# Two-layer graph attention kernel on one core: count plans read ahead, the attention fold's weights loaded by head, the second projection's first block in other banks, one eviction a chunk earlier

## The chip, the cores and the metric

The kernel runs on one core of a Trainium2 chip, in one launch. The metric is the device time of an execution in microseconds, lower is better. Three executions of the kernel before took 921.67, 923.18 and 926.49 us.

## The reference

Two graph attention layers over 1250 nodes of 768 values and 20000 edges (plus one self loop a node), a residual and a layer norm:

```
def _gat_layer(x, src, dst, W, a_src, a_dst, bias, concat):
    h = (x @ W).reshape(N, H, C)
    al_s = einsum('nhc,hc->nh', h, a_src);  al_d = einsum('nhc,hc->nh', h, a_dst)
    e = leaky_relu(al_s[src] + al_d[dst], 0.2)
    ex = exp(e - segment_max(e, dst)[dst])
    alpha = ex / (segment_sum(ex, dst)[dst] + 1e-16)
    out = segment_sum(h[src] * alpha[:, :, None], dst)
    ...                                   # heads side by side, or their mean
h   = elu(_gat_layer(x, src, dst, W1, att_src1, att_dst1, b1, concat=True))   # 4 heads of 512
out = _gat_layer(h, src, dst, W2, att_src2, att_dst2, b2, concat=False)       # 1 head of 768
return layernorm(x + out)
```

## The kernel before, in words

There is no gather. The edges are counted into a dense matrix C of 1250 x 1250 (source block x target), and each layer is a dense product: for a source block of 125 nodes and a half of the targets (a *chunk*, 125 x 625) the weights exp(...) x counts are made, split into a high and a low part, and multiplied with the rows of h, each product in three passes (high x high, high x low, low x high). Each engine runs its own list of instructions written out by hand, and semaphores order them; there is no scheduler. The stages in the order of TensorE's list (`block.tensor`):

1. *Fold*: W1 is transposed in 16 steps (`fold_step(i)`, four a head: six transposes, L1791, then two products of the step before with the attention vectors, L1801). ScalarE copies the transposes out (`weights_out`, L1102). Ten steps (`FS`) stand ahead of the counts, the rest between the first count windows. `w1f` holds W1 for this; the sync engine SP issues its loads as 12 DMAs of two heads each. ScalarE makes its share of the one-hots (`slot_ones`, L1062 and L1065) before its first `weights_out`.
2. *Counts*: 30 windows of 41 or 42 targets. VectorE makes one-hots (`one_hots`, L1422, seven a step), TensorE multiplies them (`window`, L1854 to L1863, in a loop whose trip count is data), ScalarE copies the counts out (`strip_out`, L1077) and makes the table for a later window (`shift_table`, L1071). Where a window's slots start and how many steps it takes is computed on VectorE (`plan_row`, semaphore `ranges`) and read into registers of TensorE and of VectorE by `windows_plan`, one read (L567) for four windows (`WQ`). The first `Q0` = 4 reads stand ahead, on TensorE ahead of the first fold step; those for windows 16, 20, 24 and 28 stand in the loop over windows. Between the windows stand transposes of x (L1822), score rows, count transposes (`transpose_counts`, L1872, with ScalarE's `mask_out`, L1085) and, from window 24 on, the split of W1's first head (ScalarE L1052, VectorE L1397).
3. *First projection and heads*: `h_block` for head 0, then 80 chunks, with `make` for the next head between them. The accumulators of five target blocks fill banks 0 to 5. `evict_group` on VectorE (L1481 to L1495) takes them out and counts `v_done`. The hidden rows go to HBM and come back as `hblk`.
4. *Second projection*: for each of ten blocks b, two halves n = 2b, 2b + 1: `transpose_h(n)` (eight transposes, L1952, into `ht_banks(n)`), split by ScalarE (L1190) and VectorE (L1507, semaphore `ht_lo`), then `mm_half(n)` (48 matmuls into `h2_banks(b % 2)`, which is banks 0, 1 or 2, 3). `h2_out(b)` on ScalarE takes the block out and counts `h2_sb`. Transposes of halves 0 and 1 stand between the last chunks of the heads. W2's last eight pieces are split meanwhile (ScalarE `split_w2`, L1195; VectorE `lo_w2`, L1555).
5. *Second aggregation*: 20 chunks in two groups of targets. For each, ScalarE (L608), GpSimd (L623), ScalarE (L630), VectorE (L636), ScalarE (L645) and VectorE (L650) work in turn. The first group's five tiles share banks 0 to 7, the second group's tiles wait (`y_b`) until `evict2` (L1700 to L1712) has taken out the tiles whose banks they use: the first one waits for tiles 0 and 1. `evict2(0)` and `evict2(1)` stand in VectorE's loop over the chunks, `norm` follows.

Of the kernel before, what the change touches and what calls it, by code (L numbers as in the profile page):

```python
# [20 lines left out]
ACT = mybir.ActivationFunctionType  # L21
# [5 lines left out]
B = 125  # L27
NB = N // B
PAIRS = E // (2 * B)
D = 768  # L30
H = 4
HC = 512
KD = D // 128
# [5 lines left out]
DH = D // 2  # L39
# [19 lines left out]
LG = 8  # L59
LV, LA = 18, 2  # L60
WQ = 4
Q0 = 4
PACK = 256
TR = 3
WRING = 2
# [4 lines left out]
FU = 16  # L70
# [5 lines left out]
GT = NB // 2  # L76
GN = GT * B
NG = 2 * H
CHUNKS = NG * NB
# [47 lines left out]
def gat_kernel(nc, x, src, dst, W1, as1, ad1, b1, W2, as2, ad2, b2, out):  # L127
# [11 lines left out]
    with ExitStack() as ctx:  # L139
        def sem(name):  # L140
            return ctx.enter_context(nc.semaphore(name))
# [62 lines left out]
        w1f = sb("w1f", [128, H, KD, HC], F32)  # L204
# [84 lines left out]
        h2f = sb("h2f", [B, NB, D], F32)  # L289
# [48 lines left out]
        PS = ctx.enter_context(nc.psum_tensor("ps", [128, 8, BANK], F32))  # L338
# [4 lines left out]
        ld_x = [sem(f"ld_x{i}") for i in range(NB // XL)]  # L343
        ld_w1 = sem("ld_w1")
        ld_an = sem("ld_an")
        ld_wf = [sem(f"ld_wf{i}") for i in range(2)]
        xT_stored = sem("xT_stored")
        ld_b1 = sem("ld_b1")
        ld_xr = [sem(f"ld_xr{i}") for i in range(XR)]
# [34 lines left out]
        ranges = sem("ranges")  # L384
# [48 lines left out]
        v_done = sem("v_done")  # L433
# [8 lines left out]
        ht_lo = sem("ht_lo")  # L442
# [106 lines left out]
            else:  # L549
                eng.wait_ge(w2_lo, c - W2F + 1)  # L550

        def h2_banks(s):

            return PS[0:B, 2 * s:2 * s + 2, 0:DH]

        def ht_banks(n):

            return (4, 5) if n % 2 and n > 1 else (6, 7)

        def ht_part(half, part, a):  # L560

# [102 lines left out]
        def _(sp):  # L664
# [2 lines left out]

            sp.dma_start(an[0:FU, :], as1.rearrange("h (t p) -> (h t) p", p=128)).then_inc(ld_an, 16)
            sp.dma_start(an[FU:2 * FU, :], ad1.rearrange("h (t p) -> (h t) p", p=128)).then_inc(ld_an, 16)
            for i in range(2):  # L670
                for k in range(KD):
                    sp.dma_start(w1f[:, 2 * i:2 * i + 2, k, :], W1[k * 128:(k + 1) * 128, 2 * i * HC:(2 * i + 2) * HC]
                                 .rearrange("p (h c) -> p h c", h=2)).then_inc(ld_wf[i], 16)

            for i in range(NB // XL):
                for lo, hi in ((0, XP), (XP, B)):
# [366 lines left out]
        def _(act):  # L1043
# [181 lines left out]

            def h2_out(b):
                act.wait_ge(h2_ps, 2 * b + 2)
                act.activation(h2f[:, b, :].rearrange("p (a n) -> p a n", a=2), h2_banks(b % 2), ACT.Copy).then_inc(h2_sb, 1)

            split_hT(0)  # L1230
            act.wait_ge(pt_lo, CHUNKS)
# [63 lines left out]
        def _(dve):  # L1295
# [442 lines left out]
                    dve.tensor_scalar(y[:, n, lo:hi], y[:, n, lo:hi], mv[:, n, 0:1], rstd[:, n:n + 1], ALU.subtract, ALU.mult).then_inc(y_done, 1)  # L1738

            for c in range(CHUNKS, CHUNKS + 2 * NB):  # L1740
                if c == CHUNKS + 2 * NB - 3:
                    evict2(0)
                    evict2(1)
                if c > CHUNKS:
                    dve_lo(dve, c)
                if c + 1 < CHUNKS + 2 * NB:
                    dve_counts(dve, c + 1)
                if c + 1 < CHUNKS + NB:
                    split_h2(c + 1 - CHUNKS)
# [20 lines left out]
        def _(pe):  # L1770
# [10 lines left out]
            def fold_step(i):  # L1781

                if i < FU:
                    if i % (FU // 2) == 0:
                        pe.wait_ge(ld_wf[i // (FU // 2)], 16 * KD)
                    if i == 1:
                        pe.wait_ge(plan, 8)
                    if i >= 2:
                        pe.wait_ge(wt_sb, i - 1)
                    for k in range(KD):  # L1790
                        t = pe.transpose(fold_banks(i)[:, k // 3, k % 3 * 128:(k % 3 + 1) * 128],  # L1791
                                         w1f[:, i // 4, k, i % 4 * 128:(i % 4 + 1) * 128], ident[:, :])
                    t.then_inc(wt_ps, 1)
                if i >= 1:
                    u = i - 1
                    if u == 0:
                        pe.wait_ge(acz_done, 1)
                        pe.wait_ge(ekeys, 2)
                    pe.wait_ge(wt_sb, u + 1)
                    for a in range(2):  # L1800
                        t = pe.matmul(PS[0:2 * H, (WRING, 7)[a], 0:DH], acz[:, u, :], wT[:, u % 2, a * DH:(a + 1) * DH],  # L1801
                                      start=u == 0, stop=u == FU - 1)
                    if u == FU - 1:
                        t.then_inc(wrow_ps, 1)
# [3 lines left out]
                         ).then_inc(keys_ps, 1)  # L1808
            pe.wait_ge(keys_red, 1)
            pe.transpose(PS[0:1, 6, 2 * PAIRS:2 * PAIRS + 2 * NW], kred[:], ident[0:2 * NW, 0:2 * NW]).then_inc(keys_row, 1)  # L1810
            pe.wait_ge(ranges, 1)
            ahead = [windows_plan(mybir.EngineType.PE, q) for q in range(Q0)]
            for i in range(FS):
                fold_step(i)

            def transpose_x(j):
                if j % XL == 0:
# [127 lines left out]
            def transpose_h(n):  # L1945
                b, half = n // 2, n % 2
                if half == 0:
                    pe.wait_ge(ld_hb[b % 2], RS * (b // 2 + 1))
                if n >= 1:
                    pe.wait_ge(ht_lo, max(n - 1, min(n, 2)))  # L1950
                for k in range(KH):
                    t = pe.transpose(PS[:, ht_banks(n)[k // 4], (k % 4) * B:(k % 4 + 1) * B],  # L1952
                                     hblk[:, b % 2, (half * KH + k) * 128:(half * KH + k + 1) * 128], ident[0:B, 0:B])
                t.then_inc(ht_ps, 1)
# [45 lines left out]

            def mm_half(n):
                b, half = n // 2, n % 2
                pe.wait_ge(ht_lo, n + 1)
                for k in range(KH):
                    c = half * KH + k
                    if n == 2 * NB - 3 and k == LATE_S:
                        pe.wait_ge(dot_done, 2 * len(PP) + 1)
                        pe.wait_ge(ht_lo, 2 * NB - 1)
                        spread(lambda m: al2[:, 0, m:m + 1], lambda m: (6, (m - NB + 3) * B), NB - 3, NB).then_inc(bc2_ps, 1)
                    if n == 2 * NB - 1 and k == LATE_G:  # L2010
                        pe.wait_ge(g_done, H + 1)
                        spread(lambda m: gcol[:, H * NB + m:H * NB + m + 1], four_from(4), 0, GT).then_inc(bc2_ps, 1)
                    if b == 0:
                        w2_lo_done(pe, c)
                    for a in range(2):
                        t = products(h2_banks(b % 2)[:, a, :],
                                     ((hT[half][:, 0, k, :], hT[half][:, 1, k, :]),
                                      (W2p[:, c, 0, a * DH:(a + 1) * DH], W2p[:, c, 1, a * DH:(a + 1) * DH])),
                                     c == 0, c == KC - 1)
                t.then_inc(h2_ps, 1)  # L2020

            for b in range(NB):
                if b == 0:
                    pe.wait_ge(v_done, H * NB - GT + 3)
                elif b == 1:
                    pe.wait_ge(v_done, H * NB)
                else:
                    pe.wait_ge(h2_sb, b - 1)
                mm_half(2 * b)
                if b + 1 < NB:  # L2030
                    transpose_h(2 * b + 2)
                mm_half(2 * b + 1)
                if b == 0:
                    pe.wait_ge(v_done, H * NB)
                if b + 1 < NB:
                    transpose_h(2 * b + 3)
            pe.wait_ge(hx_one, 2)
# [58 lines left out]
```

## Time and profile before

| | us |
|---|---|
| median of three executions | 923.18 |
| the profiled execution, as the device timed it | 924.97 |
| its span, first to last instruction | 922.9 |
| TensorE busy (matmul) in the span | 873.8 |
| VectorE, ScalarE, GpSimd busy | 621.3, 422.2, 205.4 |

The profile is of one execution. Its page gives busy times, a chain of waits followed back from the last instruction, and groups of instructions by line; the trace behind it can be asked for a stretch, an engine or a line. An engine's idle time matters only where it stands on the path that sets the end. PE is TensorE's matmul side, PEld its weight loads, a "q" behind an engine's name its sequencer, which waits, branches and reads registers. "Issue" as a releaser means that no semaphore of another engine is seen to end the wait.

### The profile page before, as it was taken

The numbers are of one execution on the slowest core, as the hardware profiler recorded it, in microseconds if no ns is written. First come the engines' busy times: TensorE is split into PE (matmuls) and PEld (weight loads), VectorE is DVE, ScalarE is ACT, GpSimd is POOL, SyncE is SP. The second block draws the span as 40 slices with busy tenths as digits, with TensorE's granted clock in tenths as the row PEclk, the third lists the DMA queues.
The fourth block names the chain that finished last, engine by engine and source line by source line (L and its number), as shares of the span: only waits on it lengthen the run. The fifth ranks groups of instructions, "written<-read, shape, count | busy, mean of one in ns | idle before, by whom it ended". The sixth has DMA issues, their size and how long they took to land.

```text
span 922.9 us, 15201 instructions
## 1 busy us (share of the span) xinstructions
PE 873.8 (95%) x5693; PEld 790.9 (86%) x5693; DVE 621.3 (67%) x1215; ACT 422.2 (46%) x681; POOL 205.4 (22%) x133
## 2 busy tenths in 40 slices
PE   4998879999999999999999999999999999999797
PEld 2456557799888998889988899989999999999796
DVE  8457663758893798937989279674122346797886
ACT  5356452166643676336664367853111111587300
POOL 1000000045322253222431234400000000154452
PEclk9999998999999999999999999999999999999899
DMA  8609897462576416774156534438123354050223
GB/s 299 149 15 135 174 183 147 150 167 94 187 252 186 147 48 202 236 198 136 48 164 215 133 127 136 128 121 193 51 73 67 70 76 99 1 121 9 76 83 93
DMA packets 71265, 119.72 MB, mean 130 GB/s; under 512 B 35660, under 2 KB 37352, under 8 KB 69818
## 3 DMA queue, kind: packets, MB, share of 16 engines
q1 hardware_dynamic: 71193, 118.76, 48.8%
q8 instruction: 46, 0.75, 0.4%
q14 instruction: 26, 0.21, 0.1%
HBM read 93.77 MB, written 24.96 MB: 129 GB/s over the span
## 4 chain that ended last, share of the span: by engine, by line
PE 69%; DVE 10%; issue 9%; POOL 6%; ACT 3%; DMA 1%; DVEq 0%; SPq 0%; POOLq 0%; ACTq 0%
PE ps L1831 19%; PE ps L1833 19%; PE ps L1832 19%; POOL pbuf L623 6%; PE ps L1860 4%; PE ps L1801 2%; PE ps L1952 2%; PE ps L1791 1%; DVE h2f L1738 1%; DVE pbuf L636 1%; DVE h2f L1712 1%; DMA w1f<-in_L_gnn_W 1%; DVE bnst L1729 1%; DVE vbuf L1495 1%; DVE vbuf L1494 1%
## 5 line engine op out<-in xcount | busy, mean ns | idle before, releaser
L623 POOL TENSOR_TENSOR pbuf<-pbuf,grow 125x625 f32<-125x625 f32 x99 | 177.4, 1793 | 680.9 <-ACT pbuf L608 244.3
L1831 PE MATMUL ps<-hx,PThi 125*125 125x260 f32 (+5 forms) x800 | 227.4, 284 | 2.8 <-DVE vbuf L1495 2.2
L1833 PE MATMUL ps<-hx,PTlo 125*125 125x260 f32 (+5 forms) x800 | 225.4, 282 | 0.0
L1832 PE MATMUL ps<-hlo,PThi 125*125 125x260 f32 (+4 forms) x800 | 224.9, 281 | 0.0
L1831 PEld LDWEIGHTS ps<-hx,PThi 125*125 125x125 f32 x800 | 148.7, 186 | 6.8 <-DVE vbuf L1495 2.7
L1832 PEld LDWEIGHTS ps<-hlo,PThi 125*125 125x125 f32 x800 | 149.1, 186 | 1.4
L1833 PEld LDWEIGHTS ps<-hx,PTlo 125*125 125x125 f32 x800 | 149.0, 186 | 0.0
L1831 PE MATMUL ps<-W2p,hT 128*125 128x384 f32 x320 | 109.9, 343 | 2.1 <-DVE vbuf L1495 2.1
L630 ACT ACTIVATE pbuf<-pbuf,s_sl 125x625 f32<-125x625 f32 x100 | 81.3, 813 | 59.1 <-POOL pbuf L623 57.0
L1833 PE MATMUL ps<-W2p,hT 128*125 128x384 f32 x320 | 108.1, 338 | 0.0
L1832 PE MATMUL ps<-W2p,hT 128*125 128x384 f32 x320 | 108.0, 338 | 0.0
L636 DVE SCALAR_TENSOR_TENSOR pbuf<-pbuf,counts 125x625 f32<-125x625 f32 x100 | 87.1, 871 | 29.4 <-ACT pbuf L630 29.2
L645 ACT ACTIVATE PThi<-pbuf 125x625 fp32r<-125x625 f32 x80 | 57.8, 722 | 107.2 <-DVE pbuf L636 65.2
L650 DVE TENSOR_TENSOR PTlo<-pbuf,PThi 125x625 fp32r<-125x625 f32 x80 | 84.4, 1055 | 28.2 <-ACT PThi L645 28.2
L1507 DVE TENSOR_TENSOR hT<-ps,hT 128x500 fp32r<-128x500 f32 x40 | 25.3, 673 | 89.0 <-ACT hT L1190 89.0
L1831 PE MATMUL ps<-h2x,PT 125*125 125x384 f32 (+9 forms) x250 | 77.5, 310 | 6.2 <-DVE h2f L1712 5.6
L1190 ACT ACTIVATE hT<-ps 128x500 fp32r<-128x500 f32 x40 | 21.3, 586 | 129.1 <-PE ps L1952 129.1
L608 ACT ACTIVATE pbuf<-drow,s_up 125x625 f32<-125x625 f32 x100 | 80.2, 804 | 0.0
L1833 PE MATMUL ps<-h2x,PT 125*125 125x384 f32 (+9 forms) x250 | 77.0, 308 | 0.0
L1832 PE MATMUL ps<-h2lo,PT 125*125 125x384 f32 (+7 forms) x250 | 76.9, 308 | 0.0
L1833 PE MATMUL ps<-W1hi,xr 128*125 128x512 f32 x180 | 71.1, 395 | 0.0
L1831 PE MATMUL ps<-W1hi,xr 128*125 128x512 f32 x180 | 71.0, 395 | 0.0
(193 smaller groups left out, 1577.2 us busy)
## 6 DMA issues: line engine op xcount, KB each, us to landing
xr<-xT_scratch SPq DMA_DIRECT2D x30, 750.0 KB, 6.6
nbm<-mask_scratch SPq DMA_DIRECT2D x40, 273.4 KB
hidden_scratch<-vbuf SPq DMA_DIRECT2D x40, 224.0 KB
hblk<-hidden_scratch SPq DMA_DIRECT2D x10, 896.0 KB
xT_scratch<-xa SPq DMA_DIRECT2D x20, 375.0 KB, 10.5
w1f<-in_L_gnn_W SPq DMA_DIRECT2D x12, 512.0 KB, 9.5
w1raw<-in_L_gnn_W SPq DMA_DIRECT2D x4, 1536.0 KB, 7.3
wf<-in_L_gnn_W SPq DMA_DIRECT2D x16, 384.0 KB, 4.4
```

What stands on the lines that cost most here:

```text
L608: act.activation(pslot(c), src[:, g * GN:(g + 1) * GN], ACT.Relu, scale=UP, bias=bias).then_inc(z_done, 1)
L623: pool.tensor_tensor(pslot(c), pslot(c), src[:, g * GN:(g + 1) * GN], ALU.add).then_inc(e_done, 1)
L630: act.activation(pslot(c), pslot(c), ACT.Exp, scale=SLOPE, bias=bias).then_inc(p_done, 1)
L636: dve.scalar_tensor_tensor(pslot(c), pslot(c), 1.0, C[:, b, g * GN:(g + 1) * GN], ALU.min, ALU.mult).then_inc(pc_done, 1)
L645: act.activation(hi_slot(c), pslot(c), ACT.Copy).then_inc(pt_hi, 1)
L650: dve.tensor_tensor(lo_slot(c), pslot(c), hi_slot(c).bitcast(F32), ALU.subtract).then_inc(pt_lo, 1)
L1190: hi = act.activation(ht_part(n % 2, 0, a), PS[:, bank, 0:4 * B], ACT.Copy)
L1507: lo = dve.tensor_tensor(ht_part(n % 2, 1, a), PS[:, bank, 0:4 * B], ht_part(n % 2, 0, a).bitcast(F32), ALU.subtract)
L1831: pe.matmul(dst, ahi, bhi, start=start, stop=False, skip_group_check=shared)
L1832: pe.matmul(dst[:, 0:n], ahi, blo, start=False, stop=False, skip_group_check=shared)
L1833: return pe.matmul(dst, alo, bhi, start=False, stop=stop, skip_group_check=shared)
L1860: t = pe.matmul(win_bank(w), oh_lo[:, bass.ds(at_slot(first, i, v), 1), :].rearrange("p o n -> p (o n)"), ring[:, w % 2, v, 0:win_cols(w)] ...
```

## The change

`Q0` becomes 8, so all eight reads of plans stand ahead of the first window on both engines. On TensorE they no longer stand ahead of the fold, but one behind each of the fold steps 1 to 8. W1 for the fold is loaded by head, two DMAs a head instead of twelve DMAs of two heads each, and fold steps 0, 4 and 8 wait for head 0, for head 1, and for heads 2 and 3. The second projection's block 0 accumulates in banks 6 and 7; the transposes of half 2 go to banks 4 and 5; so `mm_half(0)` waits for both split halves and no longer for evictions. `transpose_h(4)`, the next in banks 6 and 7, waits for block 0 to be out. On VectorE `evict2(0)` moves one chunk ahead.

```diff
-Q0 = 4
+Q0 = 8
...
-        ld_wf = [sem(f"ld_wf{i}") for i in range(2)]
+        ld_wf = [sem(f"ld_wf{i}") for i in range(3)]
...
-        def h2_banks(s):
+        def h2_banks(b):
-            return PS[0:B, 2 * s:2 * s + 2, 0:DH]
+            lo = 6 if b == 0 else 2 * (b % 2)
+            return PS[0:B, lo:lo + 2, 0:DH]
         def ht_banks(n):
-            return (4, 5) if n % 2 and n > 1 else (6, 7)
+            return (4, 5) if n in (2, 3) or (n > 3 and n % 2) else (6, 7)
...
-            for i in range(2):
-                for k in range(KD):
-                    sp.dma_start(w1f[:, 2 * i:2 * i + 2, k, :], W1[k * 128:(k + 1) * 128, 2 * i * HC:(2 * i + 2) * HC]
-                                 .rearrange("p (h c) -> p h c", h=2)).then_inc(ld_wf[i], 16)
+            for h in range(H):
+                for k in range(0, KD, KD // 2):
+                    sp.dma_start(w1f[:, h, k:k + KD // 2, :], W1[k * 128:(k + KD // 2) * 128, h * HC:(h + 1) * HC]
+                                 .rearrange("(k p) c -> p k c", p=128)).then_inc(ld_wf[min(h, 2)], 16)
...
-                if c == CHUNKS + 2 * NB - 3:
-                    evict2(0)
-                    evict2(1)
+                if c in (CHUNKS + 2 * NB - 4, CHUNKS + 2 * NB - 3):
+                    evict2(c - CHUNKS - 2 * NB + 4)
...
-                    if i % (FU // 2) == 0:
-                        pe.wait_ge(ld_wf[i // (FU // 2)], 16 * KD)
+                    if i % (FU // H) == 0 and i // (FU // H) < 3:
+                        pe.wait_ge(ld_wf[i // (FU // H)], (32, 32, 64)[i // (FU // H)])
...
-            pe.wait_ge(ranges, 1)
-            ahead = [windows_plan(mybir.EngineType.PE, q) for q in range(Q0)]
+            ahead = []
             for i in range(FS):
                 fold_step(i)
+                if i == 1:
+                    pe.wait_ge(ranges, 1)
+                if 1 <= i <= Q0:
+                    ahead.append(windows_plan(mybir.EngineType.PE, i - 1))
...
                 if n >= 1:
-                    pe.wait_ge(ht_lo, max(n - 1, min(n, 2)))
+                    pe.wait_ge(ht_lo, max(n - 1, min(n, 3)))
+                if n == 4:
+                    pe.wait_ge(h2_sb, 1)
...
-                pe.wait_ge(ht_lo, n + 1)
+                pe.wait_ge(ht_lo, max(n + 1, 2))
...
             for b in range(NB):
-                if b == 0:
-                    pe.wait_ge(v_done, H * NB - GT + 3)
-                elif b == 1:
-                    pe.wait_ge(v_done, H * NB)
-                else:
+                if b >= 2:
                     pe.wait_ge(h2_sb, b - 1)
                 mm_half(2 * b)
+                if b == 0:
+                    pe.wait_ge(v_done, H * NB)
                 if b + 1 < NB:
                     transpose_h(2 * b + 2)
                 mm_half(2 * b + 1)
-                if b == 0:
-                    pe.wait_ge(v_done, H * NB)
```

## Rows read from the trace of the kernel before

**Rows 1.** The page's chain that ended last: shares of the span by engine.
```profile
PE 69%; DVE 10%; issue 9%; POOL 6%; ACT 3%; DMA 1%; DVEq 0%; SPq 0%; POOLq 0%; ACTq 0%
```

**Rows 2.** Chain in order of time, the start: start us, us, what.
```profile
5.39 9.07 DMA w1f<-in_L_gnn_W
...
15.75 2.79 PE ps L1791 x12
18.54 1.91 PE ps L1801 x4
20.45 0.81 PE ps L1791 x6
21.26 1.39 PE ps L1801 x4
```

**Rows 3.** Timeline of ScalarE, 9 to 21: start us, us, operation, [idle before].
```profile
13.19 1.13 ACT L1065 ACTIVATE oh_lo<-oh_lo,one 125x1000 bf16<-125x1000 bf16 x1
17.30 0.81 ACT L1102 ACTIVATE wT<-ps 128x768 f32<-128x768 f32 x1 [2.98 <-PE ps L1791]
```

**Rows 4.** Line 567 around four plan reads: ns min/median/max, first and last start.
```profile
L567 PEldq TENSOR_LOAD <-rng_i x4: 1214/1236/1423, 10.4 to 14.5; - x4
...
L567 PEldq TENSOR_LOAD <-rng_i x1: 3351/3351/3351, 108.4 to 108.4; - x1
...
L567 PEldq TENSOR_LOAD <-rng_i x1: 3742/3742/3742, 121.8 to 121.8; - x1
...
L567 DVEq TENSOR_LOAD <-rng_i x8: 1161/1305/2518, 16.0 to 137.2; - x8
```

**Rows 5.** Timeline of PE at windows 20 and 24.
```profile
111.80 0.36 PE L1854 MATMUL ps<-zcols,ident_b 125*125 125x410 bf16 x1 [1.36 <-issue]
...
125.60 0.58 PE L1854 MATMUL ps<-zcols,ident_b 125*125 125x420 bf16 x1 [2.81 <-issue]
126.07 2.71 PE L1860 MATMUL ps<-ring,oh_lo 125*125 125x420 bf16 x7
```

**Rows 6.** Timeline of VectorE at windows 24 and 28.
```profile
123.28 0.33 DVE L1422 TENSOR_SCALAR ring<-table,ekey 125x420 bf16<-125x420 uint16 x1 [2.52 <-issue]
...
139.76 0.33 DVE L1422 TENSOR_SCALAR ring<-table,ekey 125x420 bf16<-125x420 uint16 x1 [1.77 <-issue]
```

**Rows 7.** Timeline of PE at window 28.
```profile
138.64 0.36 PE L1854 MATMUL ps<-zcols,ident_b 125*125 125x420 bf16 x1 [1.61 <-ACT counts L1077]
140.85 2.70 PE L1860 MATMUL ps<-ring,oh_lo 125*125 125x420 bf16 x7 [1.85 <-DVE ring L1422]
```

**Rows 8.** Stretches: us, busy by engine, granted PE clock, DMA share, GB/s.
```profile
139.00:145.80 6.80, 4.95 (x15) 3.33 (x16) 3.51 (x14) 0.54 (x1) 0.00 (x0) 0.50 1.20 173
614.50:806.00 191.50, 191.50 (x1165) 190.61 (x1165) 83.07 (x239) 45.53 (x78) 3.45 (x2) 1.00 0.39 84
855.30:866.00 10.70, 5.14 (x16) 5.14 (x17) 9.54 (x15) 4.66 (x7) 7.43 (x5) 0.68 0.24 72
866.00:916.00 50.00, 50.00 (x286) 49.93 (x284) 42.04 (x82) 1.27 (x2) 20.51 (x18) 1.00 0.28 85
```

**Rows 9.** Timeline of VectorE, PE and ScalarE at the second projection's start.
```profile
609.90 1.26 DVE L1507 TENSOR_TENSOR hT<-ps,hT 128x500 fp32r<-128x500 f32 x2 [3.16 <-ACT hT L1190]
...
614.38 0.44 PE L1831 MATMUL ps<-W2p,hT 128*125 128x384 f32 x1 [2.12 <-DVE vbuf L1495]
...
628.99 0.85 ACT L1195 ACTIVATE W2p<-w2late 128x768 fp32r<-128x768 f32 x1 [1.73 <-DVE W2p L1555]
```

**Rows 10.** Timeline of VectorE and PE between the last stage's groups.
```profile
855.31 1.34 DVE L650 TENSOR_TENSOR PT<-pbuf,PT 125x625 fp32r<-125x625 f32 x1 [0.79 <-ACT PT L645]
...
857.97 1.27 DVE L1712 SCALAR_TENSOR_TENSOR h2f<-ps,rden,xres 125x256 f32<-125x256 f32 x3
...
860.86 0.68 PE L1831 MATMUL ps<-h2x,PT 125*125 125x384 f32 x1 [5.64 <-DVE h2f L1712]
```

More of the change, by code:

```diff
@@ L1227, in h2_out @@
                 act.wait_ge(h2_ps, 2 * b + 2)
-                act.activation(h2f[:, b, :].rearrange("p (a n) -> p a n", a=2), h2_banks(b % 2), ACT.Copy).then_inc(h2_sb, 1)
+                act.activation(h2f[:, b, :].rearrange("p (a n) -> p a n", a=2), h2_banks(b), ACT.Copy).then_inc(h2_sb, 1)
             split_hT(0)
@@ L2015, in mm_half @@
                     for a in range(2):
-                        t = products(h2_banks(b % 2)[:, a, :],
+                        t = products(h2_banks(b)[:, a, :],
                                      ((hT[half][:, 0, k, :], hT[half][:, 1, k, :]),
```

## The prediction, made before the changed kernel ran

> **What bounds the kernel now.** I read the chain of waits first, then PE's waits, then the stretches. TensorE carries 69% of the chain, no other engine over 10% [rows 1]. From 614.5 to 806 us and from 866 to 916 us it has no idle time at a full clock [rows 8]. So time is to be had only where PE stands still, and an edit is worth what it takes from such a place, plus the half clock that may follow. The change touches four: the start, where the fold begins at 15.75 us [rows 2]; windows 20, 24 and 28 of the counts, where "issue" or a late VectorE holds PE [rows 5 to 7]; 2.12 us ahead of the second projection [rows 9]; 5.64 us between the last stage's two groups [rows 10]. What lies behind each is a list that PE works off, whose side chains start from PE's own instructions, so I let a gain at one place pass to the end in full.
>
> **The start.** W1's sixth DMA ends the chain's piece at 14.46 us (5.39 + 9.07), and PE starts at 15.75, because the four plan reads on its sequencer run from 10.4 to 14.5 + 1.2 = 15.7 us [rows 2, 4]. Both go: head 0 is half of what was waited for, so it is there by some 10 us (the transfers land in turn), and no read stands ahead. What is late next is ScalarE: it makes one-hots until 13.19 + 1.13 = 14.32 [rows 3] and only then copies the first transposes, 0.81 us a step [rows 3]. The transposes of steps 0 and 1 (2.79 us at the slow start) fit ahead of that. So the first product goes from 18.54 to about 15.15, 3.4 us sooner [rows 2]. Loads by head cost nothing more: SP has fewer issues, x comes behind as before, and heads 2 and 3 are wanted eight steps of 2.2 us later.
>
> The eight reads now stand in the fold. A step is 0.81 + 1.39 = 2.20 us of PE [rows 2]. The sequencer can hand over the products of step i - 1 as soon as ScalarE's copy is done, about 0.9 us behind those transposes. PE then still has the products before (1.39), the transposes (0.81) and these products (1.39) to do, 3.6 us in all from the same point, so a read has about 2.6 us of cover. One costs 1.21 to 1.42 us on an idle PE; between the windows two cost 3.35 and 3.74 [rows 4]. Bounds: nothing at all, or 8 x 1.1 = 9 us if each is as long as the longest. I take nothing, since the short rows are those of the same place in time. On VectorE eight reads from 16.0 at 1.2 to 2.5 us end between 25.7 and 36.1, the usual value of 1.3 giving 26.4; window 0 is wanted on PE at about 34.5. Sum for the start: -3.4.
>
> A rule of the Trainium skill can be set beside this, "TensorE: Matmul & The Clock Gate", in "Architectural detail: the array is 16x 32x32, not 1x 128x128": TensorE's queue holds 64 instructions, those of ScalarE and VectorE 8. By it a fold step's ten matmuls and their weight loads fit in the queue and the reads run beside them, which gives the sum above; with a queue that had to be empty the slower rival below would hold. The trace has a read that starts at 121.8 while PE works until 122.8, but it ends after PE has run dry, so it does not settle it.
>
> **Windows 16 to 28.** Window 20: PE is idle for 1.36 us, as the read from 108.4 ends at 111.75, and the first products are slower (0.38) [rows 4, 5]. VectorE's one-hots for it are early. -1.7, bounds -1.75 and 0.
>
> Window 24: PE idles 2.81 us for the read that ends at 125.55 [rows 4, 5]. Behind it the clock is at half: the seven matmuls take 2.71 us, about 1.3 more than they would at the full clock [rows 5]. VectorE also comes late, its ring at 123.28 behind its own read [rows 6]; without that it can begin about 1.5 us sooner, at 121.8, in time. So window 24 would end at 122.79 + 1.6 = 124.4 instead of 128.8, 4.4 sooner. Next in line is VectorE with the one-hots of 25 and the two splits of W1, which then carry the shift on as about 4.05. Bounds: -1.4 (half the idle time, clock still low) and -4.45.
>
> Window 28: VectorE's ring starts at 139.76, behind a read on its sequencer that begins at 137.2; the work ahead ends at 138.0 [rows 6]. Without the read it starts at about 138.05, -1.7, and PE's second wait of 1.85 us goes nearly whole; the first one, 1.61 us for ScalarE, stays [rows 7]. From 139.0 to 145.8 the clock is at half [rows 8], in which PE is busy for 4.95 us. If it stays high, half of that is saved, some 2.4 us; the idle time ahead of this drop is halved but not gone, so I take -1.2 (bounds 0 and -2.4). Window 16 gives nothing: ScalarE's table is late there too.
>
> **The second projection.** PE is through with the heads at 612.25 and waits for `vbuf` until 614.38. Now `mm_half(0)` waits for the two split halves only, and VectorE has these at 609.90 + 1.26 = 611.16 [rows 9]. -2.12. Next late: the last split piece of W2. ScalarE takes it at 628.99 [rows 9], VectorE 0.9 us later; with PE 2.1 us ahead but ScalarE's copies of half 2 only 1.4 ahead, this piece comes at 629.4 against 629.0 wanted: +0.4. The added wait of `transpose_h(4)` for block 0's exit falls more than 6 us after that exit and is free; that of half 3 for half 2's split likewise. -1.7, bounds -2.1 and 0.
>
> **The last stage.** The first tile of group two waits for tiles 0 and 1, whose evictions (about 1.6 us each, 1.27 of it the three large instructions) stand one behind the other [rows 10]. One of them moves ahead of a VectorE instruction for which VectorE idled 0.79 us anyway [rows 10]. So it fills 0.8 and pushes the other 0.8 on; with a little lost at the handovers y_b reaches 2 about 1.0 us sooner. The chunk it delays is wanted by PE ten us later. The clock is low behind this gap (0.68 in the stretch [rows 8]); I leave that as it is, since at window 24 it was low after 2.81 us of idle already, and 4.6 remain here. -1.0, bounds -1.6 and +0.5 (chunk 17 late, and through it ScalarE and GpSimd).
>
> **Sum.** -3.4 - 1.7 - 4.05 - 1.7 - 1.2 - 1.7 - 1.0 = -14.75 us, against the profiled execution's 924.97: 910.2. The median of the three runs lies 1.8 below that execution, which would give 908.4. I say 910.
>
> **Rivals.**
> (a) The reads in the fold are partly open. If each takes 3.35 to 3.74 us, 0.75 to 1.1 us of a step shows, 6 to 9 us: 916 to 919. For it: the rows of 3.35 and 3.74. Against: the four of 1.2.
> (b) Slower: a read holds until PE's queue has run dry. At window 20 it ends 1.36 us behind PE's last matmul and at window 24 2.8 us behind it [rows 5]. With that in eight fold steps PE stands for 11 to 22 us, and if the clock is low behind each wait, as at window 24, up to 8 x 2.2 = 17.6 us more. From 1.85 us a step the whole gain is gone; at 2.8 it is 22.4 - 14.75 = +7.7, 933, and with the half clock up to 950. Against it: the reads ahead of window 16 leave PE almost no idle time.
> (c) The counts don't give it. The DMA share is 1.20 while the masks and x are stored [rows 8], and ScalarE's masks wait for the stores of two blocks before. If these decide once PE is 5 us ahead, the 8.6 us of windows 20 to 28 shrink to some 3: 916.
> (d) Only the removed waits count and the clock falls in the same places (windows 24 and 28): 3.4 + 1.7 + 2.8 + 1.7 + 1.7 + 1.0 = 12.3, 912.6; this is within the forecast's own range.
>
> Chances: forecast (905 to 914) 0.60, (a) 0.15, (b) 0.08, (c) 0.17. Low end: all terms at their better bounds, about -18, from 923.2 to 925: 905 to 907; one us for the runs' spread. High end: (a) and (c) in their nearer halves, 917. A measurement of this kernel tells about 0.5% (4.6 us) from no change. Faster than 918.6 are the forecast, (c) and most of (a): 0.86. Within: the rest of (a) and a little of (b): 0.08. Slower: 0.06.
>
> **What would show it.** First products at about 15.2 and window 0 at about 34.5, PE without gaps in fold steps 2 to 9 (L1791 and L1801 each 2.2 us apart); reads of line 567 in 15 to 33 us at under 2.6 us; no "issue" ahead of windows 20 and 24; one-hots of window 28 right behind the split of W1; a full clock behind window 24; no wait for `vbuf` ahead of the second projection, and a W2 wait under 0.5 us; the gap ahead of group two at 4.6 us. The prediction is wrong if the fold shows gaps, or if the first `h_block` starts less than 8 us earlier.

## The result, and the profile after

| | before | after |
|---|---|---|
| median, same chip, four executions each | 924.46 | 914.14 (911.86 to 915.77) |
| ratio of the two, with its interval | | 0.9888 (0.9864 to 0.9911) |
| the profiled execution / its span | 924.97 / 922.9 | 914.54 / 912.5 |
| TensorE busy in the span | 873.8 | 875.3 |

Faster by 10.3 us (10.4 from one profiled execution to the other) where 14.75 were forecast from the profiled execution; the predicted 910.0 lies 4.1 below the median. TensorE's busy time did not fall (some of its work ran at half clock, other work did not): what was gained is idle time. By stage, from the starts of the same instructions in the two traces (us):

| stretch | before | after | change | predicted |
|---|---|---|---|---|
| start to the first product of window 0 | 37.91 | 36.02 | -1.9 | -3.4 |
| window 0 to the first `h_block` | 108.72 | 103.87 | -4.9 | -8.65 |
| first `h_block` to the first chunk | 45.91 | 45.94 | 0.0 | 0 |
| first chunk to the second projection | 421.84 | 419.66 | -2.2 | -2.1 |
| second projection to second aggregation | 186.12 | 186.63 | +0.5 | +0.4 |
| second aggregation to the end | 122.40 | 120.38 | -2.0 | -1.0 |

So each stretch behind `h_block` was forecast to about a microsecond, and the miss lies ahead of it. First the stretches (columns as in [rows 8]: length, busy of PE, PEld, DVE, ACT, POOL, granted PE clock, DMA share, GB/s).

```profile
15.20:19.30 4.10, 4.10 (x11) 1.48 (x12) 4.10 (x5) 0.53 (x1) 0.00 (x0) 1.00 1.05 396
63.70:67.10 3.40, 3.40 (x12) 2.31 (x12) 1.20 (x6) 0.32 (x1) 0.00 (x0) 0.50 0.00 0
73.90:77.40 3.50, 3.44 (x13) 2.58 (x14) 3.31 (x13) 1.14 (x4) 0.00 (x0) 0.51 1.20 193
132.00:138.80 6.80, 4.39 (x14) 2.96 (x15) 4.72 (x16) 2.00 (x5) 0.00 (x0) 0.50 1.19 176
848.80:855.60 6.80, 4.68 (x15) 4.68 (x16) 5.72 (x10) 4.15 (x6) 4.73 (x3) 0.50 0.34 109
855.60:905.00 49.40, 49.40 (x282) 49.40 (x281) 41.43 (x81) 0.73 (x1) 22.55 (x19) 1.00 0.29 86
```

The half clock (1.2 of 2.4 GHz) behind window 24 is gone, the one at window 28 has stayed, and two stretches at 63.7 and 73.9 are new; the kernel before showed 1.00 from 36 to 80 us. Next PE at the start, which answers to [rows 2].

```profile
9.85 2.82 PE L1791 MATMUL ps<-ident,w1f 128*128 128x128 f32 x12 [2.03 <-DMA w1f<-in_L_gnn_W]
15.17 2.72 PE L1801 MATMUL ps<-wT,acz 128*8 128x384 f32 x4 [2.50 <-ACT wT L1103]
17.82 1.54 PE L1791 MATMUL ps<-ident,w1f 128*128 128x128 f32 x6
19.29 1.46 PE L1801 MATMUL ps<-wT,acz 128*8 128x384 f32 x4
20.68 0.88 PE L1791 MATMUL ps<-ident,w1f 128*128 128x128 f32 x6
...
34.63 1.46 PE L1801 MATMUL ps<-wT,acz 128*8 128x384 f32 x4
36.02 0.39 PE L1857 MATMUL ps<-zcols,ident_b 125*125 125x420 bf16 x1
```

The transposes start 5.9 us sooner, the first product 3.3 sooner and at the forecast moment. Then step 1 takes 4.12 us (15.17 to 19.29) and all later ones 2.2. Four products take 2.72 us against 1.46 later, six transposes 1.54 against 0.88: durations of the low clock, although the window above says 1.00 (no change of the clock is recorded before 19.3; the trace of `c_mask`, below, does record one there). All the eight reads are in the fold (ns min/median/max, first and last start), and PE shows no gap at them:

```profile
L568 PEldq TENSOR_LOAD <-rng_i x8: 759/1226/1427, 15.2 to 31.2; - x8
L568 DVEq TENSOR_LOAD <-rng_i x8: 731/1166/1410, 16.0 to 25.1; - x8
```

PE from window 20 to window 29, which answers to [rows 5, 7]:

```profile
109.54 0.34 PE L1857 MATMUL ps<-zcols,ident_b 125*125 125x410 bf16 x1
...
119.88 0.34 PE L1857 MATMUL ps<-zcols,ident_b 125*125 125x420 bf16 x1
120.07 1.74 PE L1863 MATMUL ps<-ring,oh_lo 125*125 125x420 bf16 x7
...
125.42 1.72 PE L1863 MATMUL ps<-ring,oh_lo 125*125 125x410 bf16 x7 [1.24 <-DVE ring L1423]
...
134.41 2.70 PE L1863 MATMUL ps<-ring,oh_lo 125*125 125x420 bf16 x7 [4.14 <-DVE ring L1423]
137.35 2.10 PE L1863 MATMUL ps<-ring,oh_lo 125*125 125x410 bf16 x7
```

Both waits of "issue" are gone. But PE then waits 4.14 us in one piece at window 28, where it had waited 1.61 + 1.85. The chain of waits in order of time (start us, us, what) says what for, and ScalarE's and VectorE's timelines at that place give the steps:

```profile
121.73 8.48 DMA mask_scratch<-nbs
...
130.29 1.00 ACT nbs L1086
```

```profile
130.29 1.00 ACT L1086 ACTIVATE nbs<-ps 125x1000 bf16<-125x1000 f32 x1 [2.52 <-DMA mask_scratch<-nbs]
...
131.45 1.15 ACT L1053 ACTIVATE W1hi<-w1raw 128x512 fp32r<-128x512 f32 x2
```

```profile
132.12 1.29 DVE L1398 TENSOR_TENSOR W1lo<-w1raw,W1hi 128x512 fp32r<-128x512 f32 x2 [2.76 <-ACT W1hi L1053]
133.33 2.90 DVE L1423 TENSOR_SCALAR ring<-table,ekey 125x420 bf16<-125x420 uint16 x11
```

`nbs` has two buffers. ScalarE may write the next mask only when the store of the mask two blocks before has landed. That store was issued at 120.4 and landed at 130.2. ScalarE's split of W1 stands behind the mask in its list, VectorE's second half of the split behind that, and the one-hots of window 28 behind that: a late DMA reaches TensorE through three engines. In the kernel before, this mask was written at 134.87 without a wait.

The second projection, answering to [rows 9] (PE, ScalarE, PE):

```profile
605.49 0.34 PE L1834 MATMUL ps<-W2p,hT 128*125 128x384 f32 x1
...
622.70 0.45 PE L1834 MATMUL ps<-W2p,hT 128*125 128x384 f32 x1 [0.19 <-DVE W2p L1556]
```

```profile
620.81 0.85 ACT L1196 ACTIVATE W2p<-w2late 128x768 fp32r<-128x768 f32 x1 [1.74 <-DVE W2p L1556]
```

The wait for `vbuf` is gone. Between the last stage's groups, answering to [rows 10] (VectorE, then PE):

```profile
846.45 1.27 DVE L1713 SCALAR_TENSOR_TENSOR h2f<-ps,rden,xres 125x256 f32<-125x256 f32 x3
847.63 0.80 DVE L651 TENSOR_TENSOR PT<-pbuf,PT 125x625 fp32r<-125x625 f32 x1
...
849.60 1.27 DVE L1713 SCALAR_TENSOR_TENSOR h2f<-ps,rden,xres 125x254 f32<-125x254 f32 x3
```

```profile
850.92 0.68 PE L1834 MATMUL ps<-h2x,PT 125*125 125x384 f32 x1 [4.12 <-DVE h2f L1713]
```

The gap is 4.12 us and not 5.64. VectorE's L651 took 0.80 behind the moved eviction where it had been 1.34 at that place, which is the half microsecond more than forecast.

### The profile page after: what moved, and what is told of

Read it like the earlier page. It is cut to its first block, busy times and chain, and to the rows that moved or that the text cites. A ratio compares the mean times of both kernels' runs of the same rounds, so it can differ in the third digit from the quotient of the medians.

```text
span 912.5 us, 15196 instructions
## 1 busy us (share of the span) xinstructions
PE 875.3 (96%) x5693; PEld 792.1 (87%) x5693; DVE 618.7 (68%) x1215; ACT 422.3 (46%) x681; POOL 205.0 (22%) x133
## 4 chain that ended last, share of the span: by engine, by line
PE 67%; DVE 11%; issue 8%; POOL 7%; ACT 4%; DMA 1%; DVEq 0%; POOLq 0%; SPq 0%; ACTq 0%
PE ps L1834 19%; PE ps L1836 19%; PE ps L1835 19%; POOL pbuf L624 6%; PE ps L1863 3%; PE ps L1801 3%; PE ps L1957 2%; DVE h2f L1739 1%; PE ps L1791 1%; DVE pbuf L637 1%; DVE vbuf L1496 1%; DVE bnst L1730 1%; DVE vbuf L1495 1%; DMA mask_scratch<-nbs 1%; DVE vbuf L1502 1%
## 5 line engine op out<-in xcount | busy, mean ns | idle before, releaser
L651 DVE TENSOR_TENSOR PTlo<-pbuf,PThi 125x625 fp32r<-125x625 f32 x80 | 84.6, 1058 | 29.4 <-ACT PThi L646 29.4
## 6 DMA issues: line engine op xcount, KB each, us to landing
w1f<-in_L_gnn_W SPq DMA_DIRECT2D x8, 768.0 KB, 10.3
```

The lines of the kernel that those rows point to most:

```text
L651: dve.tensor_tensor(lo_slot(c), pslot(c), hi_slot(c).bitcast(F32), ALU.subtract).then_inc(pt_lo, 1)
```

## The experiments

Times are medians; the ratio is to the kernel before on the same chip. Each round of runs has its own executions of the kernel before, and the changed kernel was not run again beside the later ones. Executions of one and the same kernel differ in the mean granted clock (0.988 to 0.995 in `c_q4`), so differences under about 2 us are read from the stages of the traces and not from the medians.

### The parts alone

`p_plans` is the kernel before with the plans' part only, `p_w1` with W1's loads by head only, `p_rest` with the banks and the eviction only.

```diff
# p_plans
-Q0 = 4
+Q0 = 8
...
-            pe.wait_ge(ranges, 1)
-            ahead = [windows_plan(mybir.EngineType.PE, q) for q in range(Q0)]
+            ahead = []
             for i in range(FS):
                 fold_step(i)
+                if i == 1:
+                    pe.wait_ge(ranges, 1)
+                if 1 <= i <= Q0:
+                    ahead.append(windows_plan(mybir.EngineType.PE, i - 1))
```

> The kernel before with the plan reads alone changed: Q0 = 8, one read behind each of the fold steps 1 to 8; W1 is loaded as before. My theory (each part gives what it gives in the changed kernel, and the mask store is what limits windows 20 to 28): the fold starts when the sixth DMA has landed, at about 14.5 us instead of 15.75, reads take 1.2 to 1.4 us and leave no gap, no read is left in the windows; the first h_block starts 5 to 6 us earlier than at 146.6, the whole is 5 to 6 us faster than before. Rival (the gain of the windows needs the earlier start): under 3 us.

> The kernel before with W1 loaded by head alone; four reads stay ahead of the fold, four in the windows. My theory: nothing, 0 +- 0.5 us, because the four reads end at 15.7 us and hold the first fold step there whatever has landed. Rival (the load is worth its 3 us by itself): the first fold step at about 10 us and the whole 2 to 3 us faster.

> The changed kernel with the start put back (plan reads and W1 loads as before), so that only the banks of the second projection's first block and the eviction one chunk ahead are changed. My theory: the start of the second projection 2.1 us earlier, 0.4 to 0.5 lost again at the last piece of W2, the last group 1.5 us earlier and 0.3 more from where the clock's fall lies: 3 to 3.6 us faster than before. Rival (these gains are the start's, shifted): under 1.5 us.

| | us | ratio |
|---|---|---|
| `p_plans` | 917.62 | 0.9916 (0.9898 to 0.9933) |
| `p_w1` | 925.56 | 1.0002 (0.9986 to 1.0018) |
| `p_rest` | 922.19 | 0.9951 (0.9931 to 0.9971) |

W1 by head alone gives nothing: the fold still starts at 15.73, where the reads let it. The plans' part alone starts it at 14.43, where W1's sixth DMA lets it, 1.3 sooner; only both together take it to 9.85. `p_plans` gives 7.2 us where 5 to 6 were expected. At the first chunk it stands at 185.51 and the changed kernel at 185.83: the 4.6 us by which the two parts together start the fold sooner are all gone by then. Of these, 1.1 us are left at window 0 (37.12 against 36.02) and none at window 16 (95.15 against 95.35): between the two the changed kernel has two stretches of half clock, `p_plans` one. By the medians `p_plans` and `p_rest` make 9.9 of the 10.3 us, so W1's loads gave next to nothing in the whole. At window 28 `p_plans` has the same wait as the changed kernel:

```profile
129.81 1.00 ACT L1085 ACTIVATE nbs<-ps 125x1000 bf16<-125x1000 f32 x1 [2.27 <-DMA mask_scratch<-nbs]
```

Both reach window 28 at the same time (129.70 and 129.90), so these two runs don't tell what an earlier start would give there. `p_rest` gives -2.26 from the first chunk to the second projection, +0.54 in it and -1.55 behind it, beside the changed kernel's -2.2, +0.5 and -2.0; by its median it is 2.7 us faster, where 3 to 3.6 were expected.

### Four reads instead of eight

`c_q4` is the changed kernel with `Q0 = 4`, reads in the fold as changed.

> The changed kernel with Q0 = 4: four reads in the fold, four in the windows as before. My theory: slower than the changed kernel by the windows' share, 3 to 5 us, with idle time of 1.4 and 2.8 us ahead of windows 20 and 24 again. With the mask store as the limit the loss is smaller than the 8.6 us that I had put on windows 20 to 28. Rival (reads in the windows cost what I had said): 8 us slower.

919.49 (914.20 to 919.64), ratio 0.9938 (0.9921 to 0.9955): four of its five executions lie within 0.4 us of each other and some 5 us above the changed kernel. So by the medians the reads of windows 16 to 28 are worth about 5 us. The loads and the order of the fold with four reads are worth 2.7, against `p_rest`, which lacks them (922.19). The fifth execution, 914.20, is the profiled one, with a mean granted clock of 0.995 against 0.988 to 0.991 in the others, so its trace can't be set against the median. From window 16 to the first `h_block` it takes 47.01 us against the changed kernel's 44.54: the reads cost 5.6 up to window 28, and 3.1 of that come back behind it, as the wait of 4.14 us is not there. It has no half clock at 63 and 74 us, and behind the wait at window 24 only this:

```profile
121.69 0.36 PE L1857 MATMUL ps<-zcols,ident_b 125*125 125x420 bf16 x1 [2.12 <-issue]
122.16 1.57 PE L1863 MATMUL ps<-ring,oh_lo 125*125 125x420 bf16 x7
```

After 2.12 us of idle time the seven matmuls take 1.57 us; after 2.81 us they had taken 2.71 [rows 5]. So the half clock behind a wait is no fixed price. The idle times ahead of windows 20 and 24 are 0.56 and 2.12 us, not the 1.4 and 2.8 expected.

### The mask's store earlier

`c_mask`: the store of the mask that is waited for moves ahead of a wait in SP's list that has nothing to do with it.

```diff
+            store_nb(5)
             sp.wait_ge(rows_sb, 3)
             ...
             store_xT(6)
-            store_nb(5)
```

> The changed kernel with the store of mask 5 moved ahead in SP's list, in front of the wait for the score rows. Theory 1 (ScalarE's wait of 2.5 us for this store holds the split of W1 and window 28): the wait goes, PE's gap of 4.14 us ahead of window 28's products shrinks to about 1.6, the first h_block starts 2.5 us earlier, more if the clock then stays full; the whole 2 to 5 us faster than the changed kernel. Rival (transfers in total are the limit, whatever their order): another store is waited for instead, within 1 us of the changed kernel.

909.79, ratio 0.9833 (0.9805 to 0.9860): by the medians 4.4 us under the changed kernel. ScalarE writes the mask at once (126.88, no wait), and PE's wait at window 28 is 1.81 us:

```profile
131.00 1.95 PE L1863 MATMUL ps<-ring,oh_lo 125*125 125x420 bf16 x7 [1.81 <-DVE ring L1423]
```

From window 28 to `h_block` it takes 7.48 us against 9.99, with 3.4 us of half clock and not 6.8. This 2.5 us is what the moved store gives in this trace. It settles that the wait for the store was on the path. From window 0 to `h_block` it takes 100.64 us against 103.87, but 0.7 of that lies ahead of window 16, where this execution has one stretch of half clock and the changed kernel's has two. Two later masks do wait (0.63 and 3.10 us), and nobody waits for them.

Up to window 28 the edit changes nothing in the list of TensorE, and at the start this trace records what the changed kernel's did not, a clock that falls. First the stretch that stands above with 1.00, then PE:

```profile
15.20:19.30 4.10, 4.10 (x12) 1.61 (x13) 4.10 (x5) 1.33 (x2) 0.00 (x0) 0.64 1.05 394
```

```profile
15.16 1.58 PE L1801 MATMUL ps<-wT,acz 128*8 128x384 f32 x4 [2.60 <-ACT wT L1103]
16.67 1.54 PE L1791 MATMUL ps<-ident,w1f 128*128 128x128 f32 x6
```

### The start: what holds the first products

`c_warm` puts twelve more transposes, into a bank nobody reads, between the first transposes and the first products: extra work in the 2.50 us gap. `c_act` takes the gap away: ScalarE makes the second half of its one-hots between its copies in the fold.

```diff
# c_warm
+                        for k in range(12):
+                            pe.transpose(PS[:, 1, 0:128], w1f[:, 0, k % KD, 0:128], ident[:, :])
                         pe.wait_ge(acz_done, 1)
# c_act
...
-            for g in range(LA):
-                slot_ones(g)
+            slot_ones(0)
             for i in range(FS):
                 weights_out(i)
+                if i in (0, 2, 3):
+                    slot_ones(1, {0: (0, 2), 2: (2, 5), 3: (5, LG)}[i], False)
+                if i == 4:
+                    slot_ones(1, (0, 0), True)
```

> The changed kernel with twelve extra transposes of W1 into the unused bank 1, where TensorE waits 2.5 us for ScalarE's first copy (12.7 to 15.2 us). Theory 2 (fold step 2 ran at half clock, since TensorE stood still just ahead of it, and this cost 1.4 us): the clock is full at 15.2 to 16 us and window 0 starts 1 to 1.4 us earlier than at 36.0. Rival (the clock rises at a time of its own after the start of work, and the idle time does not matter): window 0 within 0.3 us of 36.0.

> The changed kernel with ScalarE's second group of one-hots put between its copies of fold steps 0 to 4 instead of ahead of all copies. Theory 2: ScalarE's one-hots are what TensorE waits for from 12.7 to 15.2; the first products start at about 12.4 instead of 15.2 and window 0 at about 33, 3 us earlier; of this at least 1 us is lost again to the mask store of window 26, whose transfers don't get faster: 1 to 3 us faster in the whole. Rival (another input of the fold or VectorE's one-hots of window 0 holds it): under 1 us at window 0.

`c_warm`: 912.54, ratio 0.9868 (0.9848 to 0.9887). Its PE at the start:

```profile
15.17 1.69 PE L1803 MATMUL ps<-wT,acz 128*8 128x384 f32 x4
16.79 0.88 PE L1791 MATMUL ps<-ident,w1f 128*128 128x128 f32 x6
17.59 1.46 PE L1803 MATMUL ps<-wT,acz 128*8 128x384 f32 x4
```

The products start at the same 15.17 and step 1 takes 2.42 us and not 4.12; window 0 starts at 34.32, the 34.5 of the forecast. The wait for ScalarE and the products are the same, so that 1.7 us was the clock. `c_act`: 909.69, ratio 0.9833 (0.9813 to 0.9853); products from 12.55, window 0 at 32.38. It meets the mask's store even earlier (ScalarE waits 2.87 us, PE 4.49) and is 4.5 us faster all the same, where only 1 to 3 were expected, since the store would take part of it back. It takes back 0.6 us (window 28 is 5.7 us sooner, `h_block` 5.2): the store is issued earlier too, at 116.42 and not 120.37.

`c_both` is `c_mask` and `c_act` together.

> Both of these edits together: mask store 5 ahead, and ScalarE's one-hots between the copies. If the two theories hold and are independent, the gains add: 4 to 8 us faster than the changed kernel, 906 to 910 us. If the second edit only feeds the wait that the first one takes away, no more than the larger of the two.

905.99, ratio 0.9797 (0.9778 to 0.9816). The gains of the two against the changed kernel, 4.35 and 4.45, make 8.8; together they give 8.15. No half clock is left ahead of 839 us. `c_both` and `c_act` differ in the mask's store alone and both reach window 28 at 124.17. From there to `h_block` `c_act` takes 10.56 us, with a wait of 4.49 and 6.8 us of half clock behind it, and `c_both` 6.24, with a wait of 1.76 and none. So the wait for the store is worth 4.3 us where the half clock goes with it, and 2.5 where some of it stays, as in `c_mask`.

### The last stage: idle time, clock, and who ends last

`c_tail` and `best` (on `c_both`) put seventeen matmuls, read by nothing, into the gap ahead of group two.

```diff
+            pe.wait_ge(y_b, 1)
+            for k in range(17):
+                pe.matmul(PS[0:B, 0, 0:DH], h2x[:, 0, 0:B], h2x[:, 0, 0:DH], start=True, stop=True)
             for t in range(GT):
                 pe.wait_ge(y_b, (2, 3, GT, GT, GT + 1)[t])
```

> The changed kernel with 17 matmuls more, of h2x into a bank that is free then, between the last y_b of group one and the first product of group two. Their results are read by nothing, so the output is the same; they are extra work for TensorE in its 4.1 us of idle time there. In the changed kernel the granted clock is half from 848.8 to 855.6 us, behind that gap. My theory: the half clock follows from the idle time. It took about 6.8 us, in which about 4.7 us of TensorE work ran at half speed or beside waits, so 2.0 to 2.5 us come back: about 911.9 against 914.1, and the profile shows no half clock after 848. Rival one: the clock falls anyway in that place, since the filling leaves about 1 us idle: within 0.5 us of 914.1. Rival two: the filling runs past 850.9 us and holds up group two: 0.5 us or more slower than 914.1.

> All three additions to the changed kernel: SP's store of the neighbour counts of the next window ahead of its wait for the rows, ScalarE's second group of one-hots between its copies in the fold, and the 17 filling matmuls ahead of group two. The first two together ran at 905.99 us. If the filling keeps the clock in the last stage, 2.0 to 2.5 us less: about 903.7. If the half clock there is not of the idle time, 906.0. If the filling holds up group two, 906.5 or more. Gains of the head and of the tail should add, since no wait lies across both.

912.73, ratio 0.9880 (0.9861 to 0.9900), and 906.66, ratio 0.9802 (0.9785 to 0.9818): no gain that these tell, where 911.9 and 903.7 were expected. The profile of `c_tail` shows that the clock did stay (PE, then the stretch that was at 0.50):

```profile
848.65 3.24 PE L2062 MATMUL ps<-h2x 125*125 125x384 f32 x17 [0.95 <-DVE h2f L1713]
851.82 0.45 PE L1834 MATMUL ps<-h2x,PT 125*125 125x384 f32 x1
```

```profile
848.80:855.60 6.80, 6.80 (x38) 6.56 (x39) 5.64 (x11) 5.08 (x7) 3.82 (x3) 1.00 0.39 113
```

TensorE did its part: from the start of the second aggregation to its last matmul 111.53 us against 113.64. But from there to the end it took 8.64 us against 6.74. VectorE's list at that place has no wait for TensorE any more:

```profile
905.31 0.15 DVE L1701 TENSOR_SCALAR deps<-ps 125x1 f32<-125x1 f32 x1
905.49 0.16 DVE L1703 RECIPROCAL rden<-deps 125x1 f32<-125x1 f32 x1
905.69 0.62 DVE L1713 SCALAR_TENSOR_TENSOR h2f<-ps,rden,xres 125x384 f32<-125x384 f32 x1
906.34 0.56 DVE L1717 BATCH_NORM_STATS2 bnst<-h2f 125x6 f32<-125x384 f32 x1
906.82 0.60 DVE L1713 SCALAR_TENSOR_TENSOR h2f<-ps,rden,xres 125x384 f32<-125x384 f32 x1
```

In the changed kernel the last of these waited 0.17 us for PE: the two engines reached the end together, and what TensorE alone gains there is lost. VectorE's only waits behind the last chunk are 0.66 us at each of ten tiles for GpSimd's power of a half. `c_norm` (on the changed kernel) and `best2` (on `best`) put the scaling of a tile, now `scale`, behind the statistics of the next one.

```diff
+            def scale(n):
                 dve.wait_ge(y_pow, n + 1)
...
-            norm(0)
-            norm(1)
-            evict2(5)
...
+            for e, ns in ((5, (0, 1)), (6, (2, 3)), (7, (4, 5))):
+                for m in ns:
+                    norm(m)
+                for m in ns:
+                    scale(m)
+                evict2(e)
             norm(6)
             evict2(8)
+            scale(6)
```

> The changed kernel with VectorE's last normalisations in another order: the scaling of a tile stands behind the statistics of the next one (or behind an eviction), so that GpSimd's power of a half, for which VectorE waits 0.66 us at each of ten tiles, runs beside other work. Nothing is left out or added. The 17 filling matmuls took 2.1 us from TensorE's end in the last stage, but the end of the kernel stood: VectorE's list from the last chunk to the last tile has no other idle time than these waits. My theory: in the changed kernel TensorE and VectorE reach the last tile together (its second half waited 0.17 us for TensorE), so with a faster VectorE alone TensorE decides: 0 to 0.5 us less, about 914. Rival: VectorE alone sets the end already; then up to 8 waits of 0.66 come back, 5 us, 909.

> The kernel with the three additions (counts stored earlier, one-hots between copies, filling matmuls), with the same new order of VectorE's normalisations. My theory: the filling saves TensorE 2.1 us that VectorE took back; with VectorE's waits hidden the last tile is taken out right behind TensorE's end, so the stretch from TensorE's last product to the end is 6.7 us again and not 8.6: 1.9 us less than 906.7 (or than 906.0 of the two additions alone), about 904.3. Rival: VectorE is held by something else (the slow 2.19 us scalings beside GpSimd), and the end stays at 906.0 to 906.7.

`c_norm`: 913.10, ratio 0.9870 (0.9842 to 0.9897): the same as the changed kernel. VectorE alone has time now and waits for PE, 5.78 us and 2.48 us:

```profile
896.93 0.16 DVE L1701 TENSOR_SCALAR deps<-ps 125x1 f32<-125x1 f32 x1 [5.78 <-PE ps L1839]
...
907.48 0.62 DVE L1713 SCALAR_TENSOR_TENSOR h2f<-ps,rden,xres 125x384 f32<-125x384 f32 x1 [2.48 <-PE ps L1839]
```

`best2`: 903.71 (902.57 to 904.78), ratio 0.9772 (0.9748 to 0.9796), the fastest of all. The end of the five kernels, from the starts of the same instructions (us):

| | clock kept | VectorE reordered | 2nd aggregation to last matmul | from there to the end |
|---|---|---|---|---|
| after | no | no | 113.64 | 6.74 |
| `c_tail` | yes | no | 111.53 | 8.64 |
| `best` | yes | no | 111.56 | 8.58 |
| `c_norm` | no | yes | 113.87 | 6.69 |
| `best2` | yes | yes | 111.56 | 6.80 |

Neither edit gives anything alone, both together 2 us. The new order also takes some of the scalings partly out from beside GpSimd's work (1.57 us for 2.19, below), so what VectorE gained is not the waits alone; no run tells the two apart.

## Why the prediction came out as it did

**Start, -3.4 forecast, -1.9 came.** The two waits went, the first product came at 15.17 for 15.15, and the reads were hidden for both engines, as the row of 1.2 us had it. Rivals (a) and (b) are out: no gap at any of eight reads. This is also as the rule of the Trainium skill, "TensorE: Matmul & The Clock Gate", cited there, would have it for TensorE (64 instructions in its queue). The same rule's 8 for VectorE isn't what the trace shows, if the row's start is when the read ran: its first read starts at 16.0, with at least twelve one-hots that stand ahead of it in VectorE's list still to be done. What failed is the step that took the durations of the fold from a trace where PE ran without a pause. The sum itself had PE idle from 12.67 to 15.15, and said nothing of the clock behind that. It cost 1.7 us, as `c_warm` shows.

**Windows 20 and 24, -1.7 and -4.05.** Window 20 went from its gap of 1.36 to none, window 24 from 2.81 to none with the full clock behind it. Measured from window 16 on, window 24 begins 5.9 us sooner (95.19 to 125.60 was 30.41, 95.35 to 119.88 is 24.53), for which 1.7 + 2.8 were forecast, and its seven matmuls take 1.74 us and not 2.71. These two terms were right, and 1.4 us too small.

**Windows 0 to 16, for which the prediction had no term.** They took 57.28 us before and 59.33 after, 2.05 longer, which is more than the start had gained. The two stretches of half clock at 63.7 and 73.9 account for it: in the fourteen traces this part takes 57.15 to 57.32 us where no half clock lies in it (six kernels), 58.0 to 58.7 where one of 3.4 us does (six), and 59.33 and 59.53 where two do (the changed kernel and `c_tail`).

**Window 28 and its clock, -1.7 and -1.2.** This is the step that failed: "VectorE's ring starts at 139.76, behind a read on its sequencer", and "without the read it starts at about 138.05". Once everything is some 8 us sooner, the read isn't what VectorE waits for but ScalarE's W1 split, behind a mask that waits for the store of two blocks before. That is the mechanism of rival (c), which had a chance of 0.17. From window 24 to `h_block` it took 21.03 us before and 20.01 after, 1.0 less where the rest of the 8.65, without those 4.5, makes 4.15. With the store moved it takes 17.49 (`c_mask`) and 16.25 (`c_both`), and the forecast's 16.88 lies between. So the 3.1 us missing there are the wait for the store and the half clock behind it. The clock fell at window 28 as rival (d) had it, and not at window 24.

Together: 2.05 lost ahead of window 16, 1.4 more gained up to window 24, 3.1 missing behind it make the 3.8 us between -8.65 and -4.9.

**Second projection, -1.7.** -2.2 + 0.5: right, including that W2's last piece is next late: PE waits 0.19 us for it, and ScalarE's idle time there is still 1.74 us.

**Last stage, -1.0.** -2.0 by the trace, 1.5 of it the smaller gap. Mis-sized: I let the moved eviction push VectorE's next instruction on in full, and that instruction was itself half a microsecond shorter. The other half microsecond is not in `p_rest` (-1.55), and no run says where it comes from.

**Its own test.** I wrote that the prediction is wrong if the first `h_block` starts less than 8 us earlier. It starts 6.7 us earlier, so by that test the working of the counts was wrong. The time fell in the range of 905 to 917 since the other terms held and since the range was wide enough for the 3.8 us; 914.14 lies nearer to the 916 of rival (c) than to 910. That the counts missed by no more was in part luck, as two errors of opposite sign met there.

What stays open is what decides whether a given pause is followed by half clock: 2.12 us was not in `c_q4`, 2.81 was [rows 5]; at window 28 1.81 us was in `c_mask`, 1.76 was not in `c_both`. The changed kernel and `c_norm` have the same lists up to the last stage, and one trace has two stretches of half clock between windows 0 and 16, the other has one.

## What to carry to other kernels

When an edit moves a stage several microseconds forward, ask of every DMA that a buffer waits for whether its issue moves with it; the rotating buffer of a store was the next bound here, through three engines, and one line in the sync engine's list was worth 2.5 to 4.3 us by the traces. A gain on the bounding engine's last stage is real only as long as that engine ends last: compare how long before the end its last instruction stands, before and after. Price a pause of TensorE by its length, and give what runs behind it at half clock as a range from nothing up, since pauses of nearly the same length went either way here. Where a pause can't be removed, extra matmuls in it can keep the clock. Leave room for stretches of half clock that no row of before shows: two of them cost 2 us here.

## What was not expected of the hardware

- TensorE's products after a pause of 2.50 us ran at 2.72 us for four against 1.46, with no record of a lower clock; twelve extra transposes in the pause brought them to 1.69. In `c_mask`, behind a pause of 2.60 us, they took 1.58, and the clock is recorded at half right behind them, with the next four at 2.25.
- Seventeen unneeded matmuls (3.24 us) in a pause of 4.12 us kept the clock at 1.00 where it had been 0.50 for 6.8 us.
- VectorE's scaling of 125 x 768 values (L1739) takes 0.68 us alone and 2.2 us when it starts beside GpSimd's addition of 1.84 us. In `c_tail` GpSimd's starts at 896.29 and VectorE's at 896.36:

```profile
896.36 2.18 DVE L1739 TENSOR_SCALAR h2f<-h2f,mv,rstd 125x768 f32<-125x768 f32 x1 [0.66 <-POOL rstd L1008]
...
902.01 0.68 DVE L1739 TENSOR_SCALAR h2f<-h2f,mv,rstd 125x768 f32<-125x768 f32 x1 [0.66 <-POOL rstd L1008]
```

```profile
896.29 1.84 POOL L1012 TENSOR_TENSOR xres<-xres,b2row 125x768 f32<-125x768 f32 x1
```

The Trainium skill, "SBUF — State Buffer", section "SBUF: two separate sides", says that the two engines share one pair of ports and that, where VectorE's instruction is of a kind that needs it, the one that comes first keeps the pair for its whole instruction. The rows agree in the order: VectorE's ends 0.41 us behind GpSimd's, though a scaling that began only then would end 0.68 behind. `c_norm` moves the two apart: there VectorE's scaling starts 0.70 us behind GpSimd's addition, takes 1.57, and ends 0.42 us behind it again.

```profile
867.57 1.57 DVE L1741 TENSOR_SCALAR h2f<-h2f,mv,rstd 125x768 f32<-125x768 f32 x1
```

```profile
866.87 1.85 POOL L1012 TENSOR_TENSOR xres<-xres,b2row 125x768 f32<-125x768 f32 x1
```
